# The squares of the keys folded by GpSimd, and two steps of VectorE's order changed, in a fused block of six attention and feed-forward layers

## What is computed

```python
q, k, v = split(shift_tokens(x) @ Wqkv)          # 16 heads of 64
q = q / maximum(norm(q, axis=-1), 1e-12) * q_scale   # norms over a head's 64 elements
k = k / maximum(norm(k, axis=-1), 1e-12) * k_scale
q = q * cos * scale + rotate_half(q) * sin * scale
k = k * cos / scale + rotate_half(k) * sin / scale
attn = softmax(where(mask, -max, q @ k.T * 8.0))     # 32 x 32 for each sequence and head
x = (attn @ v) @ Wo + x
x = ffn(shift_tokens(x)) + x                     # layer norm, W1, gelu gate, W2
```

## Time and profile before

| | before |
|---|---|
| median of three runs | 2846.3 us |
| the profiled execution | 2848.0 us |
| its span | 2846.2 us |
| TensorE busy | 2691.9 us (95%) |
| VectorE busy | 2600.1 us (91%) |
| ScalarE busy | 2246.7 us (79%) |
| GpSimd busy | 2116.7 us (74%) |
| granted TensorE clock, mean | 0.988 |

### The profile page before, as it was taken

One profiled execution on the slowest core, in us unless ns is written; L12 is line 12 of the kernel. 1 busy time (PEld: TensorE's weight loads), 2 busy tenths in 40 slices (PEclk: granted clock), 3 DMA queues, 4 the chain that ended last, 5 costly groups with the idle time before them and its releaser, 6 DMA issues.

```text
span 2846.2 us, 92826 instructions
## 1 busy us (share of the span) xinstructions
PE 2691.9 (95%) x36416; PEld 2060.1 (72%) x36417; DVE 2600.1 (91%) x3375; ACT 2246.7 (79%) x3776; POOL 2116.7 (74%) x1529
## 2 busy tenths in 40 slices
PE   8799978999999999999999999999999999999996
PEld 7577756777777777777777777777777777777774
DVE  7899968999999999999999999999999999999993
ACT  5799957878788787878888787888878787887873
POOL 6766658777778777778777787777787777877771
PEclk9899999999999999999999999999999999999998
DMA  1000013232223332223232232222322322322222
GB/s 57 24 2 2 1 35 76 67 76 69 67 69 75 73 73 66 69 71 75 66 79 69 66 75 71 72 67 70 76 67 68 79 62 68 72 67 58 64 66 79
DMA packets 103719, 178.41 MB, mean 63 GB/s; under 512 B 29350, under 2 KB 52708, under 8 KB 103396
## 3 DMA queue, kind: packets, MB, share of 16 engines
q1 hardware_dynamic: 102372, 174.60, 25.2%
q10 hardware_dynamic: 1152, 1.20, 0.1%
HBM read 22.62 MB, written 2.10 MB: 9 GB/s over the span
## 4 chain that ended last, share of the span: by engine, by line
PE 30%; POOL 16%; issue 15%; ACT 11%; DMA 7%; DVE 5%; SPq 1%; POOLq 0%; ACTq 0%; DVEq 0%
PE pa L843 9%; POOL spare L1446 8%; DMA kT<-spare 7%; PE px L872 5%; PE pg L982 3%; PE ps L903 3%; PE pg L960 3%; PE px L917 3%; PE pg L974 2%; POOL xs_lo L1432 2%; DVE ss L1269 2%; ACT spare L1095 2%; POOL pr L1484 2%; ACT spare L1041 1%; POOL spare L1455 1%
## 5 line engine op out<-in xcount | busy, mean ns | idle before, releaser
L1446 POOL TENSOR_TENSOR spare<-spare,qk_t 128x1024 f32<-128x1024 f32 x384 | 910.1, 2392 | 10.9 <-POOL xs_lo L1432 8.1
L843 PE MATMUL pa<-w_hi,xs_hi 128*128 128x512 f32 x1152 | 511.9, 444 | 25.3 <-issue 8.6
L1462 POOL TENSOR_TENSOR sm<-sm,inv 128x512 f32<-128x512 f32 x192 | 201.8, 1051 | 429.2 <-DVE sm L1307 361.4
L1285 DVE TENSOR_TENSOR qk_t<-pa,rot 128x1024 f32<-128x1024 f32 x384 | 464.6, 1210 | 1.6 <-ACT spare L1048 0.8
L1276 DVE TENSOR_TENSOR spare<-pa,rot 128x1024 f32<-128x1024 f32 x384 | 464.6, 1210 | 0.0
L1269 DVE TENSOR_REDUCE ss<-spare 128x16 f32<-128x1024 f32 x384 | 457.7, 1192 | 6.1 <-ACT spare L1041 5.2
L843 PE MATMUL pa<-w_hi,xs_lo 128*128 128x512 f32 x1152 | 459.2, 399 | 0.3 <-DMA pT<-prT 0.3
L843 PE MATMUL pa<-w_lo,xs_hi 128*128 128x512 f32 x1152 | 455.0, 395 | 0.0
L872 PE MATMUL px<-ident_sb,spare 128*128 128x128 f32 x3072 | 407.2, 276 | 18.8 <-POOL spare L1455 11.9
L1455 POOL TENSOR_TENSOR spare<-spare,inv 128x1024 f32<-128x1024 f32 x192 | 365.9, 1905 | 69.6 <-ACT inv L1080 65.3
L872 PEld LDWEIGHTS px<-ident_sb,spare 128*128 128x128 f32 x3072 | 340.4, 140 | 105.1 <-issue 44.6
(11 more groups left out here) (178 smaller groups left out, 5926.1 us busy)
## 6 DMA issues: line engine op xcount, KB each, us to landing
kT<-spare SPq DMA_DIRECT2D x384, 256.0 KB, 3.7
pT<-prT SPq DMA_DIRECT2D x768, 64.0 KB, 2.0
w_part<-in_Wqkv SPq DMA_DIRECT2D x40, 192.0 KB, 3.7
wo<-in_Wo SPq DMA_DIRECT2D x6, 512.0 KB, 5.5
c_h<-in_x SPq DMA_DIRECT2D x4, 512.0 KB, 9.5
spare<-in_x SPq DMA_DIRECT2D x8, 256.0 KB, 4.8
out<-spare SPq DMA_DIRECT2D x8, 256.0 KB, 2.5
wo<-in_W SPq DMA_DIRECT2D x6, 341.0 KB, 5.2
```

The lines of the kernel that those rows point to most:

```text
L843: last = pe.matmul(pa[(u + c) % 2][:, half * 512:half * 512 + 512], x[:, j * P:(j + 1) * P], w[:, at], start=(k == 0), stop=(k == 2))
L1285: dve.tensor_tensor(halves(qk_t[:, c, :]), halves(pa[(3 * j + c) % 2][:])[:, :, ::-1, :], table.unsqueeze(1).to_broadcast([P, HEADS, 2, DH ...
L1446: pool.tensor_tensor(qk_r[:, c, :], qk_r[:, c, :], qk_t[:, c, :], ALU.add)\
```

## The change

Three edits. First, the squares of the keys: GpSimd adds, in each head, the upper 32 squares onto the lower 32 in place (fold_squares_k, first in its turn for a tile), and VectorE's key sum then reads 32 and not 64 elements of each head and waits for that fold, not for square_k. Second, in VectorE's order turn_probs comes behind the query sum, not ahead of it. Third, the reciprocal of the denominators becomes a step of its own; in tiles j = 0 to 2 it comes behind rest_of_outputs, in j = 3 it stays ahead of it.

```diff
+                def sum_squares_k(i, j, back):
+                    n, j, live = tile(i, j, back)
+                    if live:
+                        dve.wait_ge(s["folded_k"], n + 1)
+                        wait_for(dve, s["floored"], n)
+                        dve.reduce_sum(ss[:, 1, :], heads(sq)[:, :, 0:DH // 2], AX.X).then_inc(s["sum_k"], 1)
...
                         dve.reduce_sum(den[:], keys(pr[:]), AX.X).then_inc(s["den_done"], 1)
+
+                def reciprocals(i, j, back):
+                    n, j, live = tile(i, j, back)
+                    if live:
                         dve.wait_ge(s["den_done"], n + 1)
...
                         maximum(i, j, 2)
+                        sum_squares_q(i, j, 0)
                         turn_probs(i, j, 3)
-                        sum_squares(i, j, 0, 0, "sq_q", "sum_q")
...
-                        sum_squares(i, j, 0, 1, "sq_k", "sum_k")
+                        sum_squares_k(i, j, 0)
...
                         denominators(i, j, 2)
+                        if j == 3:
+                            reciprocals(i, j, 2)
                         rest_of_outputs(i, j, 3)
+                        if j < 3:
+                            reciprocals(i, j, 2)
...
+                def fold_squares_k(i, j, back):
+                    n, j, live = tile(i, j, back)
+                    if live:
+                        pool.wait_ge(s["sq_k"], n + 1)
+                        low, high = heads(sq)[:, :, 0:DH // 2], heads(sq)[:, :, DH // 2:DH]
+                        pool.tensor_tensor(low, low, high, ALU.add).then_inc(s["folded_k"], 1)
...
                     for j in range(GT):
+                        fold_squares_k(i, j, 0)
                         norm_scores(i, j, 2)
```

More of the change, by code:

```diff
@@ L666, in stack @@
             qk_scale_loaded rot_ready w_hi_ready w_lo_ready xs_hi_ready xs_ready q_full k_full v_full
-            sq_q sq_k sum_q sum_k floored ln_done inv_ready
+            sq_q sq_k sum_q folded_k sum_k floored ln_done inv_ready
             cos_q cos_k sin_q sin_k rot_q rot_k norm_k tq_done tq_out tk_done tk_out v_out
@@ L1263, in _, with sum_squares_q @@
             def _(dve):
-                def sum_squares(i, j, back, c, sq_sem, sum_sem):
+                def sum_squares_q(i, j, back):
                     n, j, live = tile(i, j, back)
                     if live:
-                        dve.wait_ge(s[sq_sem], n + 1)
+                        dve.wait_ge(s["sq_q"], n + 1)
                         wait_for(dve, s["floored"], n)
-                        dve.reduce_sum(ss[:, c, :], heads(sq), AX.X).then_inc(s[sum_sem], 1)
+                        dve.reduce_sum(ss[:, 0, :], heads(sq), AX.X).then_inc(s["sum_q"], 1)
+                def sum_squares_k(i, j, back):
[4 more added lines that the diff above has]
+                        dve.reduce_sum(ss[:, 1, :], heads(sq)[:, :, 0:DH // 2], AX.X).then_inc(s["sum_k"], 1)
                 def times_cos(i, j, l, c, sq_sem, transposed, cos):
```

## The result

The changed kernel takes 2873.7 us (2871.6 to 2878.2, four runs), 1.0084 times the kernel before, with a 95% interval of 1.0068 to 1.0101: 0.84% slower. The forecast was 2875. (With the result a fourth run of the kernel before came, 2852.3 us, so that its median is now 2847.0; the two medians lie 0.94% apart, inside the interval.) The profiled execution took 2873.1 us, its span 2871.3, so the two profiled executions lie 25.1 us apart.

The account below looks back on a forecast made before the run. Bound: a circle of TensorE, ScalarE copies, key DMA and TensorE, without VectorE. 41 groups at 0.57 (23.4) plus 5 layer starts at 1.06 (5.3) give 28.7 us: 2848.0 to 2876.7 profiled, median 2875; range 2848 to 2896.

Parts of the forecast that it names:

- The fold's price: GpSimd's added fold of 512 elements: 1309 ns by neighbouring rows, 1.26 us in the queue.
- The circle and the tile: Loop of TensorE, ScalarE copies, key DMA, TensorE; the fold stalls it in j = 1, 0.57 us per ordinary group.
- the layer starts: Group 1 of a layer: folds of j = 0 and j = 1 both delay the key transposes, 1.06 us each.
- The saving on VectorE, costed at 0: VectorE's half key reduction saves 2.1 us of its work a group, worth nothing since the circle does not pass there.
- The later turn, costed at 0: turn_probs behind the query sum: probabilities up to 0.25 us late in j = 0, just in time in j = 1; 0.
- the one stall of about 0.5 us before the key transposes: Expected sign: TensorE idle about 0.5 us before the j = 2 key transposes.
- The later reciprocal, at 0: Reciprocal behind the outputs' rest in j under 3: rden 1.1 us later, GpSimd's norm_probs not held in effect; 0.
- The start, at 0: Two groups at the very start of the run, without feed-forward work, were taken to lose 0.
- VectorE as the true limit: Faster rival: VectorE sets the time, its saved 2.1 us a group come free until 0.86 is used, 2807 us; chance 0.10.
- Hidden slack on TensorE: No-change rival: TensorE hides 0.5 us or more between j = 2 transposes and next subtraction, 2846 to 2851 us; chance 0.12.
- A fold of 1.7 us or more: Much slower rival: fold at 1.7 us or more, j = 0 slips too, 2897 us and more; chance 0.12.
- Two signs of being wrong: Wrong if fold over 1.5 or under 1.1 us, transposes still on project_k's heels, or key DMA's wait shrinks.

Follow-up runs that it names:

- e12: Kernel before plus fold and half key sum in j = 1 alone and the later reciprocal, turn as before: 1.0089 times the kernel before.
- e3: Changed kernel, but in j = 1 no fold and the key sum over 64 elements: 1.0024 times the kernel before.
- e7: Changed kernel plus a second two-input GpSimd instruction of the same size behind the fold in j = 1: 1.0282 times the kernel before, 2931.5 us.
- e9: Changed kernel plus a second two-input GpSimd instruction of the same size behind the fold in j = 2: 1.0075 times the kernel before.
- e5: Kernel before with the key sum over the lower 32 squares of each head and no fold: 0.9994 times the kernel before.
- e2: Kernel before plus the fold and the half key sum, VectorE's order as before: 1.0107 times the kernel before.
- e8: Kernel before with ScalarE's two shift copies of j = 0 moved behind the key copy and the logarithm: 1.0033 times the kernel before.
- e1: Kernel before with both changes of VectorE's order, no fold, key sum over 64 elements: 1.0024 times the kernel before.
- e6: Kernel before with turn_probs behind the query sum and nothing else: 1.0042 times the kernel before.
- e4: Changed kernel with the fold and the half key sum in tile j = 1 alone: 1.0080 times the kernel before.
- e10: Kernel before with the reciprocal behind the outputs' rest in j = 0 to 2 and nothing else: 0.9994 times the kernel before.

## Why the prediction was right, and where it was not

**The fold's price.** 1309 ns were read off the neighbours in the earlier trace rows, 1289 measured. The estimate from the Trainium skill, GPSIMD Engine Reference, section "Performance versus the Vector engine", was 1.12 us; the measurement decides. The Trainium skill's rule in that section, that a two-input add is about twice as slow on GpSimd, holds here: 1.29 us for the fold, where VectorE's add of two inputs of 512 elements, one of them in PSUM, takes 0.68 (L1356 before).

**The circle and the tile.** Right, and shown: the fold of j = 1 costs 0.59 us a group where the turn is the old one (e12, forecast 0.57), those of the other tiles nothing (e3), work added in j = 1 shows in full (e7), in j = 2 not at all (e9). For the layer starts, the stretch from one L1363 to the next that holds group 1 takes 50.4 to 51.5 us before, 50.95 in the mean of five, and 52.03 to 52.10 after, 52.07 in the mean: 1.12 more, where the forecast had 1.06. In the changed kernel TensorE does wait for norm_keys there:

```profile
1675.66 1.09 PE L872 MATMUL px<-ident_sb,spare 128*128 128x128 f32 x8 [0.77 <-POOL spare L1477]
```

The size is less sure than the place, since kernels without a fold in j = 1 have means from 50.8 to 51.6 for the same stretch.

**The saving on VectorE, costed at 0.** Nearly right: e5 puts the whole of it at 0.09 us a group. The prediction said that the circle contains no VectorE instruction; it touches one. Before, the query transposes of j = 1 began 1.18 us after the scores, in e5 1.03, since px is freed by the outputs' rest on VectorE. So VectorE stands close to the circle even before the change: e2 and e8 lose time by it.

**The later turn, costed at 0.** Here the step failed, twice and with opposite signs. Without the fold it costs: 0.24 us a group (e1), 0.29 alone (e6). The prediction said that in j = 1 the probabilities land just in time; they land 0.24 us late, and since this is behind the key DMA's wait, nothing absorbs it. The mis-sized term is the start of the turn in j = 1: put at 0.7 us later, it is 1.05 later (3.26 us after the scores, 2.21 before). The 0.7 supposed that VectorE's maximum would come forward by the time saved, but VectorE stands for ScalarE's rounding first.

```profile
1556.97 0.75 DVE L1350 SCALAR_TENSOR_TENSOR fn_lo<-pg,ln_par,fn_hi 128x512 fp32r<-128x512 f32 x1 [0.43 <-ACT fn_hi L1187]
```

In TensorE's weight loads of project_v's last matmul the wait has its name:

```profile
1564.03 0.19 PEld L843 LDWEIGHTS pa<-w_hi,xs_lo 128*128 128x128 f32 x1 [0.43 <-DMA pT<-prT]
```

It does not show in the total because the two delays lie side by side between the same two points, the scores of j = 1 and the key transposes of j = 2, and the later one counts: 16.47 by the probabilities (e1), 16.64 by the fold. So the one stall of about 0.5 us before the key transposes that was forecast is not what the changed kernel shows. Of the 0.44 us, 0.24 to 0.27 have come by then with the probabilities, and the fold adds 0.17 to 0.20; the fold would have cost its full price without the turn, as e12 shows.

With the fold the later turn even saves: 49.99 in e12 against 49.87 in e4, which differ in the turn alone. In e12 VectorE stands for norm_probs at the turn of j = 0:

```profile
1546.17 0.71 DVE L1307 STREAM_TRANSPOSE prT<-pr 128x512 f32<-128x512 f32 x1 [0.19 <-POOL pr L1512]
```

Its rest of the outputs then starts 0.11 us before the scores of j = 1 and not 0.42 as in e4, px is free later, and the query transposes start at 1.24 and not at 1.03. In e2, which lacks the later turn and the later reciprocal, the stand at the turn of j = 1 is 0.81, and the period 49.97 against 49.86 after. That 0.12 is what brings the 0.59 down to the 0.46 that was measured.

For j = 0 the forecast of up to 0.25 us late, taken out of the key DMA's wait, holds: that wait went from 0.86 to 0.58, and the scores come 10.30 us after the mean subtraction as they came 10.31 before.

**The later reciprocal, at 0.** Right (e10).

**The start, at 0.** The first L1363 of the run stands at 525.4 before and its successor at 527.4 after, 2.0 later. Without any fold this point lies at 522.9 in e6 and at 526.5 in e1, so the 2 us can't be put to the change from these profiles. That stays open. The rest, 0.4 us, came back in the last groups.

**The rivals.** VectorE as the true limit is refuted by e5. Hidden slack on TensorE is refuted by the change itself: the transposes came 0.44 later and the period grew by 0.46. A fold of 1.7 us or more is refuted by its rows.

**The signs.** The fold's length, GpSimd's queue without a gap in j = 1, the period (49.86 against 49.95) and VectorE's idle time (2.54 us more a group, forecast 2.6) came as forecast. The wait before the transposes shows in the weight loads alone. Two signs of being wrong, read as they were written, did occur: the key DMA's wait shrank, and in the matmul rows the transposes still start on the heels of project_k. The first contradicted the prediction's own account, which takes up to 0.25 us out of that wait for the later turn. The second marks what was missed, that the probabilities' delay comes before the fold's.

**The total.** That 2875 and 2873.7 lie so close is in part luck. The forecast rise of the profiled execution was 28.7 us against 25.1: the period's 0.11 us, in 41 groups, makes it 4.5 too high, and the 2.0 at the start were not in it. The step from the profiled execution to the median was put at 1.7 down; after the change the median lies 0.5 above.

## What to carry to other kernels

In this kernel, work moved to an idler engine is paid by where it stands in that engine's queue, not by how full the engine is: here the fold cost 0.59 of its 1.26 us in one tile and nothing in the three others, and 1.3 us more cost all of itself in that tile and nothing in j = 2. Before moving an instruction, follow from its releaser, through all that is queued behind it, to the first instruction of the bound engine that waits for that queue; and do it for each tile of an uneven schedule, since a change that is uniform in the code need not be so in time. Two delays between the same two points don't add, so test the parts of a change one by one: a part may cost by itself and save beside another.

## What the runs showed that I had not expected

A wait that is shorter or longer on the bound engine says nothing by itself of the period: TensorE's wait for the key DMA was 0.86 us before, 0.58 after, 0.85 with the fold and the old order, while the periods were 49.40, 49.86 and 49.97. In e12, with the old turn, it is 0.58 too, because TensorE has waited 0.20 us for VectorE's key products just before, at its first matmul behind weigh_values. And a signal from ScalarE to GpSimd took 0.07 us where GpSimd was waiting (square_k ended at 1562.72, the fold began at 1562.79), half of the 0.13 that I had read from the inv to norm_keys rows.
